# One decoder layer on one core: interleaved first products, filler rows written in pieces during attention, and deviations taken ahead of all scatters

## The reference

```
x = layernorm(x + attention(x))            # 16 heads of 16, causal, q/k/v/o projections 256 x 256
x = layernorm(x + expert_by_token_id(x))   # 4 experts; each token's id chooses one
x = layernorm(x + top1_moe(x))             # 4 experts of 256 -> 1024 -> 256, a router picks the best one
```

## Time and profile before

| | us |
|---|---|
| median of 3 runs | 293.15 |
| lowest and highest run | 292.56, 294.74 |
| the profiled execution | 292.22 |
| its span, from the first to the last instruction | 290.5 |
| PE busy | 241.4 |
| DVE busy | 191.3 |
| ACT busy | 135.0 |
| POOL busy | 66.1 |

### The profile page before, as it was taken

One profiled execution on the slowest core, in us unless ns is written; L12 is line 12 of the kernel. 1 busy time (PEld: TensorE's weight loads), 2 busy tenths in 40 slices (PEclk: granted clock), 3 DMA queues, 4 the chain that ended last, 5 costly groups with the idle time before them and its releaser, 6 DMA issues.

```text
span 290.5 us, 7125 instructions
## 1 busy us (share of the span) xinstructions
PE 241.4 (83%) x2746; PEld 191.8 (66%) x2746; DVE 191.3 (66%) x425; ACT 135.0 (46%) x229; POOL 66.1 (23%) x128
## 2 busy tenths in 40 slices
PE   4769689897998988899996466996969999999970
PEld 4356466564766654567985322995859999999950
DVE  4887777866798675599897255897434556556550
ACT  4436365775676773366743160775211233333300
POOL 8500000100022344032131852000204121222222
PEclk9999799999999999999996559999898999999996
DMA  6999564222052553322259122420000000000000
GB/s 199 333 288 282 138 209 156 73 76 72 5 151 88 154 173 111 112 72 69 79 159 384 64 75 82 111 57 2 2 18 20 4 15 18 21 20 20 10 2 15
DMA packets 17424, 28.63 MB, mean 99 GB/s; under 512 B 2733, under 2 KB 12974, under 8 KB 17392
## 3 DMA queue, kind: packets, MB, share of 16 engines
q1 hardware_dynamic: 16048, 25.28, 29.3%
q0 software_dynamic: 1344, 2.90, 2.8%
HBM read 19.43 MB, written 9.50 MB: 100 GB/s over the span
## 4 chain that ended last, share of the span: by engine, by line
PE 57%; DVE 21%; issue 8%; ACT 5%; POOL 4%; DMA 3%; SPq 1%; POOLq 0%; DVEq 0%; ACTq 0%
PE ps L1285 9%; PE ps L1681 7%; PE ps L1682 7%; PE ps L1683 7%; PE ps L1698 4%; PE ps L1700 4%; PE ps L1699 4%; DVE wf_lo L795 3%; PE ps L1362 2%; POOL sorted L519 2%; DVE arena L961 2%; PE ps L1617 2%; PE ps L1358 2%; DMA ring<-wqkvT 2%; ACT wf_hi L559 1%
## 5 line engine op out<-in xcount | busy, mean ns | idle before, releaser
L1681 PE MATMUL ps<-arena,wf_hi 128*128 128x128 f16 x352 | 60.6, 219 | 0.3 <-DVE arena L1197 0.3
L1682 PE MATMUL ps<-arena,wf_hi 128*128 128x128 f16 x352 | 60.5, 218 | 0.0
L1683 PE MATMUL ps<-arena,wf_lo 128*128 128x128 f16 x352 | 60.5, 218 | 0.0
L1682 PEld LDWEIGHTS ps<-arena,wf_hi 128*128 x352 | 34.5, 98 | 0.3
L1681 PEld LDWEIGHTS ps<-arena,wf_hi 128*128 x352 | 33.9, 96 | 0.9 <-issue 0.8
L1683 PEld LDWEIGHTS ps<-arena,wf_lo 128*128 x352 | 34.0, 97 | 0.0
L1698 PE MATMUL ps<-wf_hi,arena 128*128 x88 | 25.3, 288 | 5.9 <-DVE arena L1222 3.4
L751 ACT ACTIVATE arena<-ps 128x512 f32<-128x512 f32 x22 | 13.1, 595 | 32.8 <-PE ps L1683 32.8
L795 DVE SCALAR_TENSOR_TENSOR wf_lo<-ring,wf_hi 128x1024 f16<-128x1024 f32 x17 | 20.5, 1218 | 11.0 <-ACT wf_hi L559 5.9
L1700 PE MATMUL ps<-wf_hi,arena 128*128 x88 | 25.3, 287 | 0.0
L1699 PE MATMUL ps<-wf_lo,arena 128*128 x88 | 25.3, 287 | 0.0
(11 more groups left out here) (223 smaller groups left out, 573.2 us busy)
## 6 DMA issues: line engine op xcount, KB each, us to landing
ring<-Wf SPq DMA_DIRECT2D x17, 512.0 KB, 3.7
sorted<-fill SPq DMA_DIRECT2D x1, 4515.0 KB, 22.5
arena<-Wf SPq DMA_DIRECT2D x7, 512.0 KB, 8.4
arena<-sorted SPq DMA_DIRECT2D x20, 129.0 KB, 2.4
sorted<-fill SPq DMA_DIRECT2D x1, 1161.0 KB, 6.6
ring<-xT SPq DMA_DIRECT2D x4, 256.0 KB, 4.8
X<-x_tok SPq DMA_DIRECT2D x1, 1024.0 KB, 7.7
ring<-ctxT SPq DMA_DIRECT2D x2, 512.0 KB, 3.8
```

The source lines that it names most:

```text
L1681: t.matmul(dst, hi, a_hi[p][:, k], start=k == 0, stop=False)
L1682: t.matmul(dst, hi, a_lo[p][:, k], start=False, stop=False)
L1683: last = t.matmul(dst, lo, a_hi[p][:, k], start=False, stop=k == NK - 1)
```

## The change

1. **TensorE's opening.** The first two tiles' products are no longer made one after the other behind all weights; they are written out by weight half and chunk, each behind its own wait. The product of queries and keys of tile 2 stands ahead of the first stacks. The first scores wait for tile 0 alone, and tile 1 only at their second bank; the first transposed scores wait for single stacks.
2. **Moved to POOL:** two memsets of the stacked queries, the low parts of x for batches 2 and 3, `slots` and `pick`.
3. **Row copies of batch 0:** two of four are issued by ScalarE.
4. **Expert numbers:** nine by one instruction behind `stack_T(3)`.
5. **Fills:** `sorted2` behind the loads of step 0; `sorted3` in five pieces of seven tiles behind the loads of steps 3, 4, 7, 8 and 11, with a semaphore of its own, awaited ahead of the scatters of the second part.
6. **Deviations:** all eleven `inv_std2` stand ahead of all eleven `scatter3`.

```diff
-WARM_START, WARM_GAP = 30, 8
+FILL_AT, FILL_TILES = (3, 4, 7, 8, 11), 7
+WARM_START, WARM_GAP = 24, 8
...
@@ SP
-            sp.wait_ge(fillrow, 1)
-            for scratch, rows in ((sorted2, NSA * P), (sorted3, NR3)):
-                sp.dma_start(scratch.rearrange("(n p) d -> p n d", p=P),
-                             fill[:, :].unsqueeze(1).to_broadcast([P, rows // P, ROW])).then_inc(filled, 16)
+            def pad(scratch, first, tiles_, done):
+                rows = scratch[first * P:(first + tiles_) * P, :].rearrange("(n p) d -> p n d", p=P)
+                sp.dma_start(rows, fill[:, :].unsqueeze(1).to_broadcast([P, tiles_, ROW])).then_inc(done, 16)
...
-                for k in range(4):
-                    sp.dma_start(rows[:, k], mT[b % 2][32 * k:32 * (k + 1), :]).then_inc(m_row, 16)
+                for k in range(2 if b == 0 else 4):
+                    sp.dma_start(max_row(b)[:, k], mT[b % 2][32 * k:32 * (k + 1), :]).then_inc(m_row, 16)
...
                 while n < min(used + RING, RING_CHUNKS):
                     load(n)
                     n += 1
+                if step == 0:
+                    sp.wait_ge(fillrow, 1)
+                    pad(sorted2, 0, NSA, filled)
+                elif step in FILL_AT:
+                    pad(sorted3, FILL_AT.index(step) * FILL_TILES, FILL_TILES, filled3)
@@ POOL
             pool.wait_ge(const_m, 2)
+            link(g.memset(QT[0][SLOT:P, 0::2, :].bitcast(F32), 0.0))
+            g.memset(QT[0][0:SLOT, 1::2, :].bitcast(F32), 0.0).then_inc(const_z, 1)
+            pool.wait_ge(const_z, 1)
...
+            for b in range(2, B):
+                pool.wait_ge(x_hi, b + 1)
+                pool.wait_ge(x_lo, b)
+                t = slice(b * S, (b + 1) * S)
+                g.tensor_tensor(xTv_lo[:, :, t], xT_st[:, :, t], xTv_hi[:, :, t], ALU.subtract).then_inc(x_lo, 1)
+
+            pool.wait_ge(tile_rdy, 1)
...
+            link(g.tensor_copy(pos_i[:, 0:NA], pos[:, 0:NA]))
...
-            pool.wait_ge(filled, 32)
-            pool.wait_ge(pos_rdy, 1)
+            pool.wait_ge(filled, 16)
...
+            pool.wait_ge(filled3, 16 * len(FILL_AT))
...
-            for i in range(NS - 2):
+            for i in range(NS):
                 inv_std2(i)
-            scatter3(0, 0)
-            inv_std2(NS - 2)
-            scatter3(0, 1)
-            inv_std2(NS - 1)
             for part, (first, last) in enumerate(PARTS):
-                for i in range(max(first, 2), last):
+                for i in range(first, last):
                     scatter3(part, i)
@@ ACT
             q_odds(2)
+            act.wait_ge(in_wo, 16)
+            a.activation(wo_hi, wo_st, ACT.Copy, scale=W_SCALE).then_inc(w_hi, 1)
+            act.wait_ge(mT_done, 1)
+            act.wait_ge(const_z, 1)
+            act.wait_ge(const_q2, 2)
+            for k in range(2, 4):
+                a.dma_start(max_row(0)[:, k], mT[0][32 * k:32 * (k + 1), :]).then_inc(m_half, 16)
             proj_hi(2 * TB)
             q_odds(3)
-            act.wait_ge(in_wo, 16)
-            a.activation(wo_hi, wo_st, ACT.Copy, scale=W_SCALE).then_inc(w_hi, 1)
@@ DVE
             x_low(0)
+            counts()
             for k in range(NK):
...
-            counts()
-
-            v.memset(QT[0][SLOT:P, 0::2, :].bitcast(F32), 0.0)
-            v.memset(QT[0][0:SLOT, 1::2, :].bitcast(F32), 0.0).then_inc(const_z, 1)
             x_low(1)
             dve.wait_ge(cnt_sb, 1)
             running()
             slot_tiles(0, NA)
-            slots()
...
             max_T(0)
-            x_low(2)
             proj_lo(3)
             stacks(2)
             proj_lo(2 * TB)
             stacks(3)
-            x_low(3)
@@ PE
+            def with_high(tt, k):
+                tok = slice(tt * P, (tt + 1) * P)
+                for dst, cols, _ in outputs_of(tt):
+                    t.matmul(dst, xTv_hi[:, k, tok], wqkv_hi[:, k, cols], start=k == 0, stop=False)
+                    t.matmul(dst, xTv_lo[:, k, tok], wqkv_hi[:, k, cols], start=False, stop=False)
+
+            def with_low(tt, k):
+                tok = slice(tt * P, (tt + 1) * P)
+                for dst, cols, done in outputs_of(tt):
+                    last = t.matmul(dst, xTv_hi[:, k, tok], wqkv_lo[:, k, cols], start=False, stop=k == NK - 1)
+                    if k == NK - 1:
+                        last.then_inc(done, 1)
...
                 if g == 0:
-                    pe.wait_ge(m_row, 64 * (b + 1))
+                    pe.wait_ge(m_row, rows_in(b))
+                    if b == 0:
+                        pe.wait_ge(m_half, 32)
...
             pe.wait_ge(x_lo, 1)
-            pe.wait_ge(w_lo, NK)
-            qkv(0)
+            pe.wait_ge(w_hi, 1)
+            with_high(0, 0)
             pe.wait_ge(cnt_sb, 1)
-            qkv(1)
+            with_high(1, 0)
+            pe.wait_ge(w_lo, 1)
+            with_low(0, 0)
+            with_low(1, 0)
+            pe.wait_ge(w_hi, 2)
+            with_high(0, 1)
+            pe.wait_ge(w_lo, 2)
+            with_low(0, 1)
+            with_high(1, 1)
+            with_low(1, 1)
+            pe.wait_ge(x_lo, 2)
+            qk_product(2)
             stack_T(0)
             stack_T(1)
+            value_product(2)
             pe.wait_ge(const_m, 1)
+            pe.wait_ge(const_z, 1)
             scores(0, 0)
-            pe.wait_ge(x_lo, 2)
-            qkv(2)
+            qkv(3)
             scores(0, 1)
-            qkv(3)
+            stack_T(2)
             scores(0, 2)
-            stack_T(2)
             scores(0, 3)
...
-            pe.wait_ge(tile_rdy, 1)
-            expert_numbers(4)
             pe.wait_ge(x_lo, 3)
             pe.wait_ge(maxed, 2 * NG - 1)
             qkv(2 * TB)
             stack_T(3)
-            expert_numbers(NSA)
+            pe.wait_ge(tile_rdy, 1)
+            _, experts = nc.values_load_multi_w_load_instructions(
...
```

More of the change, by code:

```diff
@@ L1295, in _, with qk_product @@
             count(7, 0, NA)
-            def qkv(tt):
+            def qk_product(tt):
                 tok = slice(tt * P, (tt + 1) * P)
@@ L1344, in scores @@
                 if g == 0:
-                    pe.wait_ge(kT_done, TB * (b + 1))
-                    pe.wait_ge(q_even, TB * (b + 1))
-                    pe.wait_ge(q_odd, TB * (b + 1))
+                    first = 1 if b == 0 else TB * (b + 1)
+                    pe.wait_ge(kT_done, first)
+                    pe.wait_ge(q_even, first)
+                    pe.wait_ge(q_odd, first)
                     if b >= 3:
@@ L1353, in scores @@
                 for bank, qt, kt in ((0, 0, 0), (1, 1, 0), (2, 1, 1)):
+                    if bank == 1 and n == 0:
+                        pe.wait_ge(kT_done, TB)
+                        pe.wait_ge(q_even, TB)
+                        pe.wait_ge(q_odd, TB)
                     if bank == 1 and n >= 1:
@@ L1372, in scores_T @@
                 if g == 0:
-                    pe.wait_ge(m_row, 64 * (b + 1))
+                    pe.wait_ge(m_row, rows_in(b))
+                    if b == 0:
+                        pe.wait_ge(m_half, 32)
                 for bank, kt, qt in ((3, 0, 0), (4, 0, 1), (5, 1, 1)):
+                    if n == 0:
+                        if bank == 4:
+                            pe.wait_ge(q_even, 3)
+                            pe.wait_ge(q_odd, 3)
+                        else:
+                            pe.wait_ge(kT_done, 3 if bank == 3 else 4)
                     if n >= 1 and bank == 3:
@@ L1470, in _ @@
             stack_T(3)
-            expert_numbers(NSA)
+            pe.wait_ge(tile_rdy, 1)
+            _, experts = nc.values_load_multi_w_load_instructions(
+                tile_i[0:1, 0, 0:NSA], engines=[pe.engine], min_val=0, max_val=E - 1,
+                skip_runtime_bounds_check_because="each is a sum of E - 1 comparisons made on the chip, 0 or 1 each")
             for step in range(STEPS):
@@ L1476, in _ @@
                     pe.wait_ge(const_q2, 2)
-                    for e in (kT_done, q_even, q_odd):
-                        pe.wait_ge(e, 2 * TB)
                 if step != 1:
```

54 lines of the change are left out of this document (29 added, 25 removed).

## The result

The changed kernel takes 282.85 us (median of 4 executions, 281.46 to 283.78) beside 292.99 for the kernel before (292.56 to 294.74): ratio 0.9639, 95% interval 0.9583 to 0.9695. The forecast was 285.7. Six more executions, in a later series, gave 284.36 (282.69 to 286.47; ratio 0.9753, interval 0.9665 to 0.9841). The profiled execution took 283.0 for a span of 281.2, 9.3 under the span before.

The account below looks back on a forecast made before the run. Bound by an opening in which engines wait for each other, and by POOL's scatters ending the second stage. Gains of 5.4 + 2.0 = 7.4 us from the median 293.15 gave 285.7; range 282.8 to 289.2.

Parts of the forecast that it names:

- Start of the products: Opening: TensorE's first product at about 7.0 instead of 9.00, both tiles done at 12.5 or 13.5.
- the ends [a, b]: Opening: two cases, fast clock after 3.2 us or only at 12.2; first maximum 17.3 [18.3], loop begins 30.8 [31.8].
- The first maxima to the transposed ones: Opening: 9.8 us (bounds 9.2 and 10.4) instead of 10.4, transposed maxima at 27.1 [28.1].
- Row copies: Before the loop: two queues, 0.63 an issue, done 28.4 [29.4] instead of 32.43, landing in 2.4.
- The expert numbers: Before the loop: one load after the stacks, lying in the time TensorE waits for the rows.
- The opening as a whole: Loop begins at 30.8 [31.8] against 36.60: 5.8 [4.8] us gained, 5.4 taken.
- The low parts of x: Opening's second stretch: on POOL they cost nothing up to 5 us; TensorE's idle 2.40 and slow clock go.
- Fills: SP's queue in attention: pieces land in 3.2 to 4.5 us; stall up to 1.3 at the last rows, 0 taken.
- a rival of 1.3 to 3.5: Last batch's row copies: one stall behind filler pieces, giving 287 to 289 us; chance 0.13.
- Deviations ahead of scatters: End of the second stage: normalisation 2.58 earlier, eleven scatters in a row; gain 1.65 to 2.05 us, 2.0 taken.
- that rival: End of second stage: each scatter takes 0.2 us more beside vector engine work, eating the tail's gain: 287.9; chance 0.08.
- The clock: Rival: idling before the first transposed score and the last stage's products drops it to 1.2 GHz: 287.2, chance 0.10.

Follow-up runs that it names:

- changed again: The changed kernel without an edit, run once more in a later series: 284.36 us beside 293.19 for the kernel before.
- fills moved: Changed kernel with the two filler pieces behind the loads of steps 7 and 8 moved behind steps 5 and 6: 282.98 us, ratio 0.9711.
- fills early: Changed kernel with both fills where the kernel before has them, on SP's queue ahead of the first row copies: 291.84 us, ratio 0.9955.
- held clock: Changed kernel with 10 and 11 filler matmuls in TensorE's two pauses of the last stage: 281.08 us, ratio 0.9594.
- low parts back: Changed kernel with the two low parts of x moved from POOL back to the vector engine: 285.12 us beside 284.36 in the same series.
- early fillers: Changed kernel with 13 filler matmuls from about 2.2 us and 32 instead of 24 behind the counts: 281.11 us, ratio 0.9588.
- the tail alone: Kernel before with all eleven deviations ahead of the eleven scatters, nothing else changed: 291.13 us beside 292.81, ratio 0.9954.

## Why the prediction was too small

The direction and the places were right. What differed between traces of the new opening, all in us: the first product of 512 columns that takes 0.22; the first maximum; from the last transposed maxima to the first sorted load; and in the last stage from the fourth tile's copy to the fifth's, and from there to the sixth's. Where a kernel is edited in that stretch, a word says so.

| run | fast from | first maximum | last rows | tiles 4 to 5 | 5 to 6 |
|---|---|---|---|---|---|
| changed | 7.05, at once | 15.50 | 24.52 | 12.50 | 13.77 |
| changed again | 6.53, at once | 14.98 | 24.43 | 12.51 | 15.04 |
| fills moved | 12.84 | 18.30 | 23.47 (moved) | 10.84 | 13.77 |
| fills early | 10.08 | 16.59 | 22.76 (none) | 10.84 | 13.76 |
| held clock | 8.20 | 15.79 | 22.76 | 10.84 (held) | 13.77 (held) |
| low parts back | 7.57 | 15.37 | 23.28 | 10.84 | 13.76 |
| early fillers | at once (fillers) | 15.41 | 23.25 | 12.51 | 15.05 |

*Start of the products: the step that failed.* The start itself came at 7.05 for 7.0. "If it lasts 3.2 us again" put both tiles at 12.5, or at 13.5 for the other end; the trace has 10.95, and this carried through to 25.17 for the transposed maxima where 27.1 was said. The term was sized by how long the slow level had lasted in the one trace, and that was misread: in the trace of the forecast products of 256 columns start 0.11 apart from 11.79 on,

```profile
11.51 0.44 PE L1285 MATMUL ps<-arena,xT_hi 128*128 128x256 f16 x2
11.79 0.27 PE L1285 MATMUL ps<-arena,xT_lo 128*128 128x256 f16 x1
11.90 0.38 PE L1285 MATMUL ps<-arena,xT_hi 128*128 128x256 f16 x2
```

and its clock record has the rise at 11.63, so the slow level lasted 2.6 us and not 3.2; by the prediction's own sum that gives 12.2 for 12.5. The rest of the miss is that one length was taken for all executions. Over six traces of the same first products the slow level lasted from nothing to 5.7 us (12.84 - 7.12), and the first maximum ran from 14.98 to 18.30: the late end of 17.3 [18.3] was met, the early one missed by 2.3. So the ends [a, b] were no bounds; a draw at which everything is fast belonged among them. The Trainium skill, "TensorE: Matmul & The Clock Gate", section Part 1, says that the number of slow matmuls at a start differs between runs of one kernel; the six traces bear it out. Fillers from 2.2 us on took the draw away in three traces of three: the clock's first rise is at 5.6 to 6.4 there and at 6.5 to 12.8 in the six without (first maximum 15.41, 15.33 and 15.37).

*The first maxima to the transposed ones.* 9.8 said, 9.67 measured. *Row copies.* ScalarE's issues took 0.6 as taken; landing was 1.8 to 2.0 and not 2.4, and the loop began 3.3 after the transposed maxima where 3.7 was said.

*The expert numbers: a second step that failed.* They were named, and priced at nothing because the new single load is covered; what the old loads had cost was never asked. In the trace of the forecast they hold nothing back that can be seen, but in the kernel before with one load the medians fall by 2.5 to 3.1 (290.0 beside 292.53 and 293.15), and the second batch's transposed maxima stand at 50.07 against 53.2 on the mean of five traces. At most 0.7 of that is the loads themselves; most of the rest is TensorE's clock, which stays at 1.00 ahead of the last stacks, and from 39 to 41, where it was at 0.50 in three of the five traces with the old loads. Why the single load keeps the clock up isn't shown.

*The opening as a whole.* 5.4 was taken. In the two profiled executions it is 7.64 (90.68 to 83.04 at the last batch's transposed maxima). Over the traces the second batch's maxima stand at 53.2 on the mean of five with the old opening and at 44.2 on the mean of four with the new one (43.57, 43.05, 46.37, 43.85): 9.0. That is somewhat too much, since the five old executions that were traced took 1.0 more on the mean than the medians of their kernels, and the four new ones 0.1 less: about 8, by that estimate, is the size of the term. The low parts of x have 0.7 of it, where the idle 2.40 and its slow clock had been named as what goes. How the rest is shared between the products, the arithmetic moved to POOL and the row copies on two queues was not run apart.

*Fills.* 0 taken, bounds 0 to 1.3, and a rival of 1.3 to 3.5 with a chance of 0.13. The first trace has 1.72, so the rival came true in it; over the eight kernels with pieces at the old places the stretch is 22.60 to 24.52, mean 23.6, against a mean of 22.9 in the seven without pieces in attention: 0.7. The place was right, the rate wrong: a piece takes 7.4 to land, not 3.2. The wait for the last rows is itself a draw: with the pieces at the same places it was 0 to 1.8 in eight traces. Moving the pieces either way won nothing.

*Deviations ahead of scatters.* 2.0 said (1.65 to 2.05); 2.27 between the traces, 1.7 between medians with the tail alone. The scatters got no longer beside the vector engine's work (1.28 apart throughout), so that rival falls. The Trainium skill, "SBUF — State Buffer", section "SBUF: two separate sides", whose rule on the shared port pair spoke for it, finds nothing here that shows it.

*The clock.* The rival feared a fall ahead of the first transposed score; there TensorE waited 1.37 and stayed at 1.00. The 1.11 of the last stage are a draw: the traced execution of before drew 12.50 and 15.16 there, the one of after 12.50 and 13.77. In thirteen traces without fillers in those pauses the first interval was 10.8 in four and 12.3 to 12.5 in nine, the second 13.8 in nine and 15.0 to 15.2 in four; in all four with fillers they were 10.8 and 13.8.

*The sum.* -7.4 against -9.3 in the two spans: 2.2 more from the opening, 0.3 from the tail, 1.1 from a draw, less 1.7 for the fills. That the miss is not larger is luck in part: what the fills cost in this trace (1.7) hid about half of what had been left out (3.6). Against medians the gain is 8.8 to 10.1. The range's low end has a slip too: its terms give 282.8 only from the profiled 292.22; from the median of 293.15, to which 285.7 refers, they give 283.7.

Open: why the last of four row copies lands late (4.1), and TensorE still waits about 1 us, when no piece of filler is under way (fills moved); two indirect scatters start there in each run, and that wasn't tried apart.

## What to carry to other kernels

One trace is one draw: before a term is taken from a stretch with the clock at its lower level, ask for the kernel without the slow stretch too, and keep both. When a part of a change is covered in the new kernel, price what it cost in the old one as well, by a run of the old kernel with that part alone: here it was worth 2.5 to 3.1 us where the one trace showed no cost. Cheap fillers in the pauses that are left (280.73 against 284.36 here, 2.8 of it in the span) are worth trying after each change that makes a chain shorter, since such a change lays bare what the old waits had covered.

## What was not expected of the hardware

- After a pause of 1.9 to 2.7 us in TensorE's work the granted clock fell to 0.50 for 3 to 4 us in some executions and not in others, also of one and the same program (the second pause of the last stage in the two traces of the changed kernel); 21 fillers in two such pauses held it at 1.00 in four traces of four.
- Row copies of 2 KB on ScalarE's queue, which held nothing else, landed no sooner behind a fill on SP's queue (8.6) than those on SP's own (8.7). The Trainium skill, "DMA: Bandwidth & Descriptors", section "Queues, rings and completion order", says that each engine takes turns between the queues that have work; the run shows no profit of it.
- A piece of filler took 7.4 us for 903 KB in attention (122 KB per us), where the whole of 4515 KB had taken 22.5 (201 KB per us).
